# A scan, attention-free blocks and an MoE on one core: the last chunk's tail on the scan's banks, a third of the products on GpSimd, preloads ahead of each Exp, and a new instruction order

## The reference

```python
# layer 1: a selective scan (D_INNER 256, 16 states)
xi, res = split(x @ in_proj_w.T)
xi = silu(causal_depthwise_conv(xi))                 # 4 taps
dt, Bm, Cm = split(xi @ x_proj_w.T)
delta = softplus(dt @ dt_proj_w.T + dt_proj_b)
h = exp(delta * A) * h + delta * Bm * xi             # over the tokens, per (feature, state)
y = (h . Cm + xi * Dp) * silu(res);  out = y @ out_proj_w.T
# layer 2: x and a weight rounded to fp8 values, one matmul, a bias
# layer 3: a scan with 16 states: delta = mean(softplus(x @ W_delta.T + b)), y = hs @ C.T + D * x
# layer 4: an MoE: softmax router, top 2 of 8 experts, capacity 512 rows in order of the tokens;
#          expert: rms, gelu(h @ Wg) * (h @ Wu) @ Wd + buf; tokens over the capacity take a small side net
```

## Time and profile before

| | |
|---|---|
| median of 3 runs | 533.63 us (529.58 to 535.17) |
| the profiled execution | 535.09 us, its span 533.3 us |
| busy: PE, DVE, ACT, POOL | 425.3, 419.7, 315.1, 178.6 us |
| mean granted TensorE clock | 0.889 |

### The profile page before, as it was taken

One profiled execution on the slowest core, in us unless ns is written; L12 is line 12 of the kernel. 1 busy time (PEld: TensorE's weight loads), 2 busy tenths in 40 slices (PEclk: granted clock), 3 DMA queues, 4 the chain that ended last, 5 costly groups with the idle time before them and its releaser, 6 DMA issues.

```text
span 533.3 us, 5892 instructions
## 1 busy us (share of the span) xinstructions
PE 425.3 (80%) x1680; PEld 256.9 (48%) x1680; DVE 419.7 (79%) x942; ACT 315.1 (59%) x517; POOL 178.6 (33%) x147
## 2 busy tenths in 40 slices
PE   4976667699649999997569999775599995449994
PEld 3322212253235778552245776432367774147883
DVE  3087999997989999698989989978899884334654
ACT  2586552378738976577578785255787832544232
POOL 0056485555163434234163433451534100000000
PEclk9987977799969999999869999969799998656997
DMA  8295768666426354442193554620835000000000
GB/s 300 109 339 175 240 210 263 211 217 202 163 79 200 116 171 161 142 160 78 32 334 133 180 167 132 220 92 20 323 151 175 23 1 1 20 0 1 0 1 20
DMA packets 22064, 74.18 MB, mean 139 GB/s; under 512 B 2320, under 2 KB 4368, under 8 KB 21648
## 3 DMA queue, kind: packets, MB, share of 16 engines
q1 hardware_dynamic: 22032, 73.82, 41.0%
HBM read 72.50 MB, written 1.31 MB: 138 GB/s over the span
## 4 chain that ended last, share of the span: by engine, by line
PE 50%; DVE 21%; issue 13%; ACT 12%; POOL 2%; DVEq 0%; ACTq 0%; POOLq 0%
PE ps_y L475 12%; PE ps_u L608 9%; PE ps_g L564 8%; DVE ps_state L919 6%; PE ps_u L564 5%; DVE product L934 3%; PE ps_state L564 2%; ACT x L703 2%; ACT ps_state L692 2%; DVE stats L944 1%; PE ps_y L608 1%; POOL drive L813 1%; PE ps_g L523 1%; DVE l_state L990 1%; PE ps_g L534 1%
## 5 line engine op out<-in xcount | busy, mean ns | idle before, releaser
L813 POOL TENSOR_TENSOR drive<-du,b_row 128x512 f32<-128x512 f32 x128 | 164.0, 1290 | 208.3 <-DVE ps_state L919 186.0
L475 PE MATMUL ps_y<-product,par 128*128 128x512 f32 x256 | 135.7, 655 | 13.2 <-DVE product L934 12.9
L692 ACT ACTIVATE ps_state<-delta,decay_rate 128x512 f32<-128x512 f32 x128 | 86.2, 687 | 63.9 <-DVE product L934 61.9
L934 DVE TENSOR_TENSOR product<-ps_state,c_row 128x512 f32<-128x512 f32 x128 | 86.1, 680 | 5.5 <-PE ps_y L475 5.3
L919 DVE TENSOR_TENSOR_SCAN ps_state<-ps_state,carry,drive 128x512 f32<-128x512 f32 x64 | 81.5, 1282 | 4.0 <-ACT ps_state L692 4.0
L475 PEld LDWEIGHTS ps_y<-product,par 128*128 128x128 f32 x256 | 48.9, 208 | 70.6 <-issue 37.3
L919 DVE TENSOR_TENSOR_SCAN ps_state<-ps_state,drive 128x512 f32<-128x512 f32 x64 | 77.3, 1219 | 2.3 <-ACT ps_state L692 2.3
L608 PEld LDWEIGHTS ps_u<-wd,hidden 128*128 128x128 f32 x448 | 54.2, 191 | 5.4 <-issue 2.4
L608 PE MATMUL ps_u<-wd,hidden 128*128 128x128 f32 x448 | 54.6, 275 | 0.0
L1092 DVE SCALAR_TENSOR_TENSOR acc<-ps_u,net_weight,acc 128x128 f32<-128x128 f32 x128 | 35.9, 344 | 15.3 <-PE ps_u L608 12.5
L774 ACT ACTIVATE gelu<-ps_g 128x512 f32<-128x512 f32 (+1 forms) x42 | 24.4, 597 | 31.8 <-PE ps_g L564 18.5
(11 more groups left out here) (199 smaller groups left out, 605.4 us busy)
## 6 DMA issues: line engine op xcount, KB each, us to landing
b_row<-bc_dram SPq DMA_DIRECT2D x64, 512.0 KB, 5.0
c_row<-bc_dram SPq DMA_DIRECT2D x64, 512.0 KB, 4.1
x_in<-x_t SPq DMA_DIRECT2D x4, 256.0 KB, 7.0
gelu<-w_gate SPq DMA_DIRECT2D x1, 1024.0 KB, 9.3
hidden<-w_up SPq DMA_DIRECT2D x1, 1024.0 KB, 10.9
wd<-w_down SPq DMA_DIRECT2D x1, 1024.0 KB, 12.8
out<-result SPq DMA_DIRECT2D x4, 256.0 KB, 2.4
par<-params SPq DMA_DIRECT2D x1, 598.0 KB, 6.7
```

Of the source, the lines that this page charges most:

```text
L475: mm(ps_y[:, :], ident, product[:, g % PRODUCTS, :], start=False, stop=(n == STATE - 1)).then_inc(y_pe, 1)
L692: nc.scalar.activation(ps_state[g % RING][:, :], delta[:, c % 2, h, :], ACT.Exp, scale=decay_rate[:, h, n:n + 1]).then_inc(decay_act, 1)
L813: nc.gpsimd.tensor_tensor(drive[:, g % DRIVES, :], du[:, h, :], b_row[:, m % ROWS, n % 2, :], ALU.mult).then_inc(drive_pool, 1)
L934: v.tensor_tensor(product[:, g % PRODUCTS, :], state[:, :], c_row[:, m % ROWS, n % 2, :], ALU.mult).then_inc(product_dve, 1)
```

## The change

It does these things.

- `MULTIPLIED` names the steps whose product GpSimd makes: steps 3, 7, ... 31 of chunk 0 (8), steps 2, 5, ... 29 of each other chunk (10). For these DVE's scan writes into `drive` and not into the bank; GpSimd multiplies (`multiply`) and in chunks 0 and 2 copies the carry. `PAIRED` is empty, so `pair` does nothing. `DRIVES` is 6, `PRODUCTS` 8. The Exp of a step whose bank was left by such a scan waits for the scan alone.
- The tail of chunk 3 uses `ps_state` and `ps_y` (`tail_bank`) and `product` for the third layer's buffers (`l1_of`). It waits for the last scan and product and no longer for the MoE of chunk 2.
- Softplus by halves: one `sp_exp` buffer; the second half's Exp waits for the first half's Ln and for DVE's `a0`. `low` has one buffer. `result` is `acc`, and ACT waits for the output's DMA before it writes `acc` anew. The third layer's state has one buffer and a carry of its own.
- `gate`, `up` and `join` are placed for each bank and not for each net.
- `preload_act_table_set(EXP_LN)` is written ahead of each step's Exp, in `rsqrt`, in each half of the softplus, and ahead of the Exp of tail pieces 7, 8 and 13; those at L651 and L776 go.
- `PLACES` is new for all engines and each chunk. On ACT and DVE all of `split` stands ahead of the first scan step. The scan of chunk 3 ends, in the order of each engine, before most of the MoE of chunk 2, and tail 3 stands between the pieces of that MoE.

```diff
-DRIVES = 5
-PRODUCTS = 5
+DRIVES = 6
+PRODUCTS = 8
+THIRD = frozenset(range(2, UNITS, 3))
+PAIRED = (NONE, NONE, NONE, NONE)
+QUARTER = frozenset(range(3, UNITS, 4))
+MULTIPLIED = (QUARTER, THIRD, THIRD, THIRD)
...
+        def tail_bank(c, name):
+
+            if c == LAST:
+                return {"r1": ps_state[0], "x1t": ps_state[1], "ffn": ps_state[2], "x2t": ps_y, "dlt": ps_state[2],
+                        "bx": ps_state[0], "mean": ps_state[1], "r3": ps_y, "hnt": ps_state[2], "logits": ps_state[1],
+                        "counts": ps_y}[name]
...
                 if k == 0:
-                    if c:
+                    if c == LAST:
+                        pe.wait_ge(product_dve, count(by_vector, STEPS - 1))
+                        pe.wait_ge(state_dve, STEPS)
+                    elif c:
                         pe.wait_ge(hidden_dve, 2 * NETS * c)
                         pe.wait_ge(gelu_act, 2 * NETS * c)
                         pe.wait_ge(acc_dve, NETS * c)
...
             def step(c, k):                      (ACT)
                 if old >= 0:
-                    act.wait_ge(product_dve, old + 1)
-                    if old // UNITS % PER_BATCH == 0:
-                        act.wait_ge(carry_dve, carries(old))
+                    if multiplied(old):
+                        act.wait_ge(state_dve, old + 1)
+                    else:
+                        made(act, old)
+                        if old // UNITS % PER_BATCH == 0:
+                            carried(act, old)
+                nc.scalar.preload_act_table_set(EXP_LN)
                 nc.scalar.activation(ps_state[g % RING][:, :], delta[:, c % 2, h, :], ACT.Exp,
                                      scale=decay_rate[:, h, n:n + 1]).then_inc(decay_act, 1)
...
             def rsqrt(marks, c, log, log_name, in_, eps_, out_):
 
+                nc.scalar.preload_act_table_set(EXP_LN)
                 do(marks, log, in_, ACT.Ln, bias=eps_)
...
             def pre(c, k):                       (ACT)
-                    if k == 3:
-                        nc.scalar.preload_act_table_set(EXP_LN)
...
-                    for h in range(HALVES):
-                        after(act, pre_act, c, f"abs{h}")
-                        do(pre_act, sp_exp[:, h, :], sp_abs[:, h, :], ACT.Exp, scale=-1.0)
-                    for h in range(HALVES):
-                        after(act, pre_act, c, f"exp{h}")
-                        do(pre_act, sp_ln[:, h, :], sp_exp[:, h, :], ACT.Ln, bias=1.0)
+                    h = k - 7
+                    after(act, pre_act, c, f"abs{h}")
+                    if h:
+                        after(act, pre_dve, c, "a0")
+                        after(act, pre_act, c, "ln0")
+                    nc.scalar.preload_act_table_set(EXP_LN)
+                    do(pre_act, sp_exp[:, :], sp_abs[:, h, :], ACT.Exp, scale=-1.0)
+                    after(act, pre_act, c, f"exp{h}")
+                    do(pre_act, sp_ln[:, h, :], sp_exp[:, :], ACT.Ln, bias=1.0)
...
+            def multiply(c, k):                  (GpSimd)
+                if not multiplied(g):
+                    return
+                pool.wait_ge(state_dve, g + 1)
+                pool.wait_ge(c_in[m % ROWS], 16 * (m // ROWS + 1))
+                if g >= PRODUCTS:
+                    added(pool, g - PRODUCTS)
+                nc.gpsimd.tensor_tensor(product[:, g % PRODUCTS, :], drive[:, g % DRIVES, :], c_row[:, m % ROWS, n % 2, :],
+                                        ALU.mult).then_inc(product_pool, 1)
+                if c % PER_BATCH == 0:
+                    nc.gpsimd.tensor_copy(carry[:, h, n:n + 1], drive[:, g % DRIVES, CHUNK - 1:CHUNK]).then_inc(carry_pool, 1)
...
-                v.tensor_tensor_scan(state[:, :], state[:, :], drive[:, g % DRIVES, :],
+                v.tensor_tensor_scan(drive[:, g % DRIVES, :] if multiplied(g) else state[:, :], state[:, :], drive[:, g % DRIVES, :],
                                      0.0 if first else carry[:, h, n:n + 1], ALU.mult, ALU.add).then_inc(state_dve, 1)
```

More of the change, by code:

```diff
@@ L84 @@
[L84 to L87, removed]
@@ L176, in build @@
         acc = sb("acc", [P, BLOCKS, P])
+        result = acc
         x1 = sb("x1", [P, BLOCKS, P])
@@ L182, in build @@
                     "wu": hidden[:, :, :, :].rearrange("p r f (e n) -> p (r f e) n", n=HIDDEN)}
[L183 to L188, removed]
+        L1_NAMES = "abs exp relu sp step decay drive"
         u = sb("u", [P, 2, HALVES, CHUNK])
         res_gate = sb("res_gate", [P, 2, HALVES, CHUNK])
-        low = sb("low", [RANK + 2 * STATE, 2, CHUNK])
+        low = sb("low", [RANK + 2 * STATE, CHUNK])
         sp_abs = sb("sp_abs", [P, HALVES, CHUNK])
-        sp_exp = sb("sp_exp", [P, HALVES, CHUNK])
+        sp_exp = sb("sp_exp", [P, CHUNK])
         sp_ln = sp_abs
@@ L203, in build, with l1_of @@
         product = sb("product", [P, PRODUCTS, CHUNK])
+        def l1_of(c, name):
+            name = {"ln": "abs", "t": "sp"}.get(name, name)
+            i = L1_NAMES.split().index(name)
+            if c == CHUNKS - 1:
+                place = product[:, i, :]
+            elif i < 6:
+                place = gelu[:, i // 2, i % 2, :]
+            else:
+                place = hidden[:, 1, 0, :]
+            return place[0:STATE, :] if name in ("step", "decay", "drive") else place
         carry = sb("carry", [P, HALVES, STATE])
@@ L335, in block_of, with multiplied, absorbed, count @@
             return ap[:, j * P:(j + 1) * P]
-        def carries(g):
-            c, k = divmod(g, UNITS)
-            return c // PER_BATCH * UNITS + k + 1
+        def multiplied(g):
+            return g % UNITS in MULTIPLIED[g // UNITS]
+        def absorbed(g):
+            return g % UNITS + 1 in PAIRED[g // UNITS]
+        def count(which, g):
+            return sum(map(which, range(g + 1)))
+        def by_pool(g):
+            return multiplied(g)
+        def by_vector(g):
+            return not multiplied(g)
+        def summed(g):
+            return not absorbed(g)
+        def paired(g):
+            return g % UNITS in PAIRED[g // UNITS]
+        def made(eng, g):
+            if multiplied(g):
+                eng.wait_ge(product_pool, count(by_pool, g))
+            else:
+                eng.wait_ge(product_dve, count(by_vector, g))
+        def added(eng, g):
+            if absorbed(g):
+                eng.wait_ge(pair_pool, count(paired, g + 1))
+            else:
+                eng.wait_ge(y_pe, count(summed, g))
+        def carried(eng, g):
+            which = by_pool if multiplied(g) else by_vector
+            eng.wait_ge(carry_pool if multiplied(g) else carry_dve,
+                        sum(which(i) for i in range(g + 1) if i // UNITS % PER_BATCH == 0))
         def blocks_of(ap):
@@ L378, in pair @@
                 if m >= ROWS:
[L379 removed]
+                    for g in (2 * (m - ROWS), 2 * (m - ROWS) + 1):
+                        used(sp, g)
                 if r == 0:
@@ L459, in pre @@
                     after(pe, pre_act, c, "low")
-                    last = mm(bank_[:, :], dt_proj[0:RANK, h * P:(h + 1) * P], low[0:RANK, q, :], start=True, stop=True)
+                    last = mm(bank_[:, :], dt_proj[0:RANK, h * P:(h + 1) * P], low[0:RANK, :], start=True, stop=True)
                 last.then_inc(pre_pe.sem, 1)
@@ L760, in tail @@
                     if c:
-                        after(act, fin_act, c - 1, "result")
+                        act.wait_ge(stored, 16 * c)
                     for j in range(BLOCKS):
@@ L764, in tail, with gate @@
                     last.then_inc(tail_act.sem, 1)
-            def gate(c, e):
+            def gate(c, i):
+                e, f = divmod(i, 2)
                 m = NETS * c + e
-                rows = P if e < EXPERTS else SIDE
-                for f in range(2 if e < EXPERTS else 1):
-                    inc = 1 if e < EXPERTS else 2
-                    act.wait_ge(gate_pe, 2 * m + f + inc)
-                    if m >= GROUP:
-                        act.wait_ge(hidden_dve, 2 * (m - GROUP) + 2)
-                    nc.scalar.activation(gelu[0:rows, m % GROUP, f, :], net_bank(c, e, "wg", f)[0:rows, :], ACT.Gelu).then_inc(gelu_act, inc)
-                if e % GROUP == GROUP - 1 and (c < LAST or e == EXPERTS):
-                    nc.scalar.preload_act_table_set(EXP_LN)
+                rows, inc = (P, 1) if e < EXPERTS else (SIDE, 2)
+                act.wait_ge(gate_pe, 2 * m + f + inc)
+                if m >= GROUP:
+                    act.wait_ge(hidden_dve, 2 * (m - GROUP) + 2)
+                nc.scalar.activation(gelu[0:rows, m % GROUP, f, :], net_bank(c, e, "wg", f)[0:rows, :], ACT.Gelu).then_inc(gelu_act, inc)
             def fin(c, k):
@@ L821, in tail, with multiply, pair @@
                                             ALU.add).then_inc(tail_pool.sem, 1)
-            run("gpsimd", du=make_du, step=step, tail=tail)
+            def multiply(c, k):
```

(24 more changed lines are left out.)

261 lines of the change are left out of this document (134 added, 127 removed), and 113 rows, old and new, of the table PLACES.

## The result

The changed kernel takes 593.3 us (median of 4 runs, 591.5 to 594.1) against 532.9 us: a ratio of 1.113 (95% interval 1.107 to 1.120), slower by 11%.

The account below looks back on a forecast made before the run. VectorE was taken as the bound, 90% busy in the scan stage, with ACT becoming the bound after the change. Head 38, scan stage 429, stretch to MoE 3 66 and MoE 3 49 gave 582, stated as 581 us; range 474 to 615.

Parts of the forecast that it names:

- (3): Table loads on ACT: 204 in place of 65, 133 of the set already loaded, 1.28 us each; ACT's work 493 us.
- The sum: Whole span: head 38, scan stage 429, last Exp to MoE 3 66, MoE 3 49, together 582 us.
- (1): 38 products moved from DVE to GpSimd: 25.8 us off DVE; POOL from 179 to some 233 us.
- (2): Contention of GpSimd with some 44 two-SBUF-input VectorE instructions: 14 us at most, covered as ACT becomes the bound.
- (4): Softplus by halves: exp1 waits for a0, some 1.2 us per chunk, 5 us over the kernel.
- (6): Order of the head: all 16 splits ahead of the first step; first Exp at about 38 us (35 to 40).
- (5): Last tail beside the third MoE: MoE 2's PE work can fill the 43 us serial stretch.
- Rival B: Loads of a set already there cost next to nothing; VectorE stays the bound, 487 us; chance 0.20.
- The threshold: In the scan stage, ACT falls below VectorE's 306 us when each redundant load costs under 0.5 us.
- C: No change: the added loads, 178 us, lie in ACT's 218 us of idle time; 528 to 550 us; chance 0.05.
- Rival D: Slower still: the ring of three banks holds up the scan stage, ACT at most 85% busy; 643 us; chance 0.05.
- The drain: The skill's 1380 ns added to a 1283 ns table load at a switch, 2.66 us; the forecast decided against it.

Follow-up runs that it names:

- e1: Changed kernel with a preload only where the Exp set is not loaded, 71 loads in place of 204: 481.5 us, ratio 0.905 to the kernel before.
- e3: Kernel before with a preload ahead of each scan step's Exp and nothing else of the change: 598.5 us, ratio 1.125.
- e4: Changed kernel with the step's preload written ahead of the step's waits, 204 loads as before: 585.2 us, ratio 1.099 to the kernel before.
- e6: e1 with tail 3 and all of MoE 3 placed behind MoE 2 on every engine: 514.3 us, ratio 0.966 to the kernel before.
- e9: e1 with the preload kept at each eighth scan step, needed or not, 84 loads: 487.0 us, ratio 0.915 to the kernel before.
- e2: e1 with the preload kept at each second scan step, needed or not, 123 loads: 514.2 us, ratio 0.964 to the kernel before.

## Why the prediction held

*Table loads (3).* The mechanism is the one forecast, and e1 (loads taken out) and e3 (loads put into the kernel before) show it from both sides. Right in count, 204, and in price, 1.283 us each also for a set that is there, a price that no row had shown and on which the direction hung. ACT's work was put at 493 us and is 498.3; of the scan stage 408 and 412. The place of the load behind the wait mattered little (e4, 8 us of 593).
*The sum.* 38 + 429 + 66 + 49 became 35.3 + 445.4 + 60.1 + 51.5. The mis-sized term is the scan stage: I took ACT to be 95% busy and it was 93%: 4 us more work and 12 us more idle time. The head and the tail were 9 us too long in the forecast and the last MoE 3 too short. These errors cancel in part, by luck: alone, the scan stage would have put the forecast 16 us too low. So the sum of 582 (the forecast says 581) became a span of 592.3.
*DVE's share (1), (2).* I expected it to lose 25.8 us and left out the 18 carries, 2.7 more. Its busy time fell by 16.3, its durations added up one by one by 29.8 (481.5 to 451.7): the products and carries are gone in full, but in the kernel before more of the instructions overlapped. Contention, for which I allowed up to 14 us, cost nothing on balance: the softplus and some small operations last longer, and the splits, which my 44 operations left out, last 6.2 us less, 0.48 us each in the head where GpSimd stands, against means of 0.63 and 1.10 before. GpSimd's carry copies took 0.19 us at the median, not 0.3, and the scans that write to SBUF 1.21 and 1.27 us, as those to PSUM.
*Softplus and head (4), (6).* The 5 us of standing did not come: ACT stood 0.7 us in all ahead of the eight loads in the softplus. The first Exp came at 35.3 us, not 38.
*The filled serial stretch (5).* Right: 60 us for both; e6 prices it at 33 us on e1.
*Rival B* described e1, where the loads aren't there: its terms 38 + 340 + 60 + 49 = 487 stand against 30.4 + 341.3 + 59.3 + 50.3 = 481.3. That 340 met 341.3 is luck: it came from 306 us of DVE work at 90%, and e1 has 325 at 95%. As a description of the changed kernel it was wrong, since a redundant load isn't free. The threshold that I gave it, ACT passing DVE, was too sharp a picture: e9 and e2 show a cost of 0.42 to 0.63 us a load while ACT is still less busy than DVE.
*Rivals C and D.* ACT's idle time of 218 us did not take in 178 us of loads, because a third of it lay elsewhere: by the earlier trace rows only 141 us of it were in the scan stage, where ACT's work rose by 145. Rival D needed ACT at 85% or less there, and it was at 93%; ahead of the 128 steps' loads it stood 12.9 us in all, so the ring of three banks did not hold it up much.
*The drain.* The Trainium skill ("ScalarE: Activation LUTs", section "What ACT_TABLE_LOAD costs") adds some 1380 ns of drain to a switch. The timelines do not have it: in the earlier trace rows the load for a switch begins 0.01 us after the end of the Silu ahead of it, and the next activation 1.30 us after the load began.

## What to carry to other kernels

Count the instructions that a call emits, not those that are needed: here a preload of an activation table that was already loaded took 1.28 us of ScalarE like any other, so keep the loaded set in a variable and load on a change. An engine's idle time over the span is no room for new work. It has to lie in the stage, and even there a part of each added microsecond was paid here, more as the engine filled. A busy time counts overlapping instructions once; to check work that moves between engines, add up the durations. When a large change is slower as a whole, take its parts one at a time: here one of them cost 112 us and hid two others worth 21 and 33, and the version without it, at 481.5 us, beats both kernels.

## What the runs showed of the hardware

A load of the set that is already loaded takes the same 1283 ns as a switch (the mean of every group of loads in the changed kernel, 204 loads, of which 133 were redundant). TensorE's mean granted clock was 0.83 in the stretched scan stage and 0.92 in that of e1 (PE busy 70% and 85% there), and PE's busy time for the same 1680 matmuls was 438 us against 408. PE was not the fullest engine of that stage, but no run separates what its lower clock cost, so a part of the 112 us may be its.

A DVE operation with two SBUF inputs took up to 1.64 us beside GpSimd where it needs 0.69. Some with one SBUF input waited too (1.21 us in place of 0.42 in e1), and GpSimd's carry copy took up to 1.12 us in place of 0.19, while DVE's products with one input in PSUM stayed at 0.66 to 0.69 us beside the same GpSimd.
